# Four graph layers with residual normalisations: one layer's low part taken earlier, one normalisation's moments kept in PSUM

## The reference

```python
x = layernorm(x + hypergraph(x, adj))      # D^-1 H B^-1 H^T (x W1^T) + b, relu, layer norm of 512, once more to 256, + x
x = layernorm(x + relu([x, adj x / deg] W^T))
x = layernorm(x + adj relu(adj relu(adj x V1 + c1) V2 + c2) V3 + c3)
t = relu((adj x) K)
x = layernorm(x + t * (any feature of the node is non-zero))
```

## Time and profile before

| | |
|---|---|
| median of 3 runs | 1506.76 us (1504.32 to 1507.04) |
| the profiled execution's own time | 1506.82 us |
| its span, first to last instruction | 1505.0 us |
| mean granted clock of TensorE | 0.986 of full speed |
| TensorE busy | 1404.5 us, 93% of the span |
| VectorE, ScalarE, GpSimd busy | 78%, 74%, 69% |
| DMA, mean | 31 GB/s |

### The profile page before, as it was taken

One profiled execution on the slowest core, in us unless ns is written; L12 is line 12 of the kernel. 1 busy time (PEld: TensorE's weight loads), 2 busy tenths in 40 slices (PEclk: granted clock), 3 DMA queues, 4 the chain that ended last, 5 costly groups with the idle time before them and its releaser, 6 DMA issues.

```text
span 1505.0 us, 34549 instructions
## 1 busy us (share of the span) xinstructions
PE 1404.5 (93%) x10896; PEld 1350.6 (90%) x10896; DVE 1173.1 (78%) x4060; ACT 1110.5 (74%) x2634; POOL 1038.1 (69%) x1096
## 2 busy tenths in 40 slices
PE   5899999999999999999999999999999999999984
PEld 5799999999999999999999999999999999999974
DVE  5678878878878878878888888888787787887763
ACT  4578777777777777777777777777777777877853
POOL 4676776776776676676676676677677677677642
PEclk8899999999999999999999999999999999999997
DMA  4001001001001101101101101101101101100000
GB/s 132 22 12 36 26 30 36 29 27 36 29 26 36 37 19 37 36 19 37 36 19 37 36 19 37 36 19 37 36 19 36 37 19 36 36 22 22 15 15 22
DMA packets 29956, 47.13 MB, mean 31 GB/s; under 512 B 3408, under 2 KB 12240, under 8 KB 29776
## 3 DMA queue, kind: packets, MB, share of 16 engines
q1 hardware_dynamic: 29776, 44.91, 9.6%
HBM read 28.12 MB, written 16.78 MB: 30 GB/s over the span
## 4 chain that ended last, share of the span: by engine, by line
PE 91%; issue 5%; DVE 2%; ACT 1%; POOL 0%; DMA 0%; POOLq 0%; ACTq 0%; DVEq 0%
PE psum L265 87%; PE psum L382 2%; PE psum L313 1%; DVE n_st L864 1%; DVE p_f L1007 0%; DVE psum L1053 0%; ACT x L574 0%; POOL BH L1258 0%; DVE n_s L1037 0%; DMA at_in<-adjT 0%; DVE psum L1027 0%; DVE x L896 0%; DVE n_mv L869 0%; ACT r_f L579 0%; DVE n_s L1176 0%
## 5 line engine op out<-in xcount | busy, mean ns | idle before, releaser
L1225 POOL TENSOR_TENSOR h_lo<-h_f,h_hi 128x512 fp32r<-128x512 f32 x128 | 166.0, 1297 | 206.1 <-ACT h_hi L555 206.1
L574 ACT ACTIVATE x<-n_s,n_shift,n_rstd 128x256 f32<-128x256 f32 x384 | 208.7, 592 | 3.6 <-DVE n_shift L886 3.2
L1233 POOL TENSOR_TENSOR r_lo<-r_f,r_hi 128x512 fp32r<-128x512 f32 x128 | 163.2, 1302 | 45.3 <-ACT r_hi L555 45.3
L265 PE MATMUL psum<-v_hi,h_hi 128*128 128x256 f32 x512 | 150.3, 294 | 6.8 <-issue 6.8
L864 DVE BATCH_NORM_STATS2 n_st<-n_s 128x6 f32<-128x256 f32 x384 | 142.4, 413 | 9.6 <-POOL n_s L1325 5.2
L1317 POOL TENSOR_TENSOR n_s<-tk,mask 128x512 f32<-128x512 f32 x64 | 66.7, 1042 | 119.5 <-issue 103.8
L265 PE MATMUL psum<-w2c_hi,r_hi 128*128 128x258 f32 x512 | 146.6, 286 | 0.0
L265 PE MATMUL psum<-w2c_lo,r_hi 128*128 128x258 f32 x512 | 145.3, 284 | 0.0
L265 PE MATMUL psum<-v_hi,h_lo 128*128 128x256 f32 x512 | 145.1, 283 | 0.0
L265 PE MATMUL psum<-v_lo,h_hi 128*128 128x256 f32 x512 | 144.8, 283 | 0.0
L265 PE MATMUL psum<-gx_hi,w1T_hi 128*128 128x256 f32 x512 | 144.5, 282 | 0.0
(11 more groups left out here) (159 smaller groups left out, 5524.8 us busy)
## 6 DMA issues: line engine op xcount, KB each, us to landing
x_in<-x_in_dram SPq DMA_DIRECT2D x64, 256.0 KB, 2.8
out<-x SPq DMA_DIRECT2D x64, 256.0 KB, 2.0
at_in<-adjT SPq DMA_DIRECT2D x64, 128.0 KB, 2.5
x<-v_in SPq DMA_DIRECT2D x3, 256.0 KB, 6.0
n_s<-w2T_in SPq DMA_DIRECT2D x2, 256.0 KB, 3.7
r_f<-w1T_in SPq DMA_DIRECT2D x2, 256.0 KB, 4.5
h_f<-wab_in SPq DMA_DIRECT2D x2, 256.0 KB, 6.2
rows<-rows_in SPq DMA_DIRECT2D x1, 256.0 KB, 6.2
```

The source lines that it names most:

```text
L265: return pe.matmul(o, a, b, start=start, stop=stop)
L574: last = act.activation(dst[:, g, :], nm.s[:, g, :], ACT.Identity, scale=nm.rstd[:, g:g + 1], bias=nm.shift[:, g:g + 1])
L1225: return pool.tensor_tensor(dst[1][:], src, f(dst[0][:]), ALU.subtract).then_inc(signal, 1)
L1233: pool.tensor_tensor(r_s[1][:, half], r_f[:, half], f(r_s[0][:, half]), ALU.subtract).then_inc(r_lo[h], 1)
```

## The change

1. `n4`'s moments lie in bank 1 (`BANK["H1"]`) in place of SBUF. So VectorE waits for `h1_relu` of pair `n - 3` before it writes them, and TensorE's `Gx` waits for `n4.shifted`.
2. ScalarE's `root(n4)` stands right behind `root(n3)`, ahead of `square_mean`; it stood behind `round_GT`.
3. VectorE's `invert(n4)` and `shift(n4)` stand right behind `shift(n3)`, ahead of `wide_var`; they stood behind `stats(n2)`.
4. VectorE takes the low part of `Ax3` right behind `sum_n2`. Behind it come `stats(n2)`, the low part of `Gx`, `moments_n2`, `sum_n1` and `stats_alone(n1)`, and only then `invert(n2)` and `shift(n2)`.
5. ScalarE rounds `Ax3` ahead of `round_GT`, and takes `H2`'s relu and rounding ahead of `root(n2)` and `apply(n4)`.

```diff
--- before.py
+++ after.py
@@ -121,7 +121,7 @@
                 self.varied, self.rooted = sem(f"{name}_varied"), sem(f"{name}_rooted")
                 self.inverted, self.done = sem(f"{name}_inverted"), sem(f"{name}_done")
         n1, n2 = Norm("n1", sums=False), Norm("n2", moments=BANK["H1W"])
-        n3, n4 = Norm("n3", moments=BANK["AP3"]), Norm("n4")
+        n3, n4 = Norm("n3", moments=BANK["AP3"]), Norm("n4", moments=BANK["H1"])
         w2T_f = [n3.s[:], n4.s[:]]
 
 
@@ -321,6 +321,8 @@
                     pe.wait_ge(r_relu[0], upto(p - 1))
                 if begun(n - 3):
                     pe.wait_ge(h1_relu, upto(n - 3))
+                if begun(n - 5):
+                    pe.wait_ge(n4.shifted, upto(n - 5))
                 propagate_T("Gx", x_in[:, k % RING], GT[k % 2])
 
             def R(n, k):
@@ -787,6 +789,8 @@
                 if active("AP3", n):
                     p = n - 4
                     root(n3, p)
+                if active("F", n):
+                    root(n4, n - 5)
                 if active("P", n):
                     square_mean(n, k)
                     root_h(n, k)
@@ -808,21 +812,12 @@
                         act.wait_ge(pe_did["H2"], upto(p - 1))
                     copy(h1w[:].rearrange("p g d -> p (g d)"),
                          psum[:, BANK["H1W"], 0:2 * D]).then_inc(h1w_out, 1)
+                if active("Ax3", n):
+                    split_hi("Ax3", ax3, ax3_hi, n - 4, pe_did["TK"])
                 if active("Tr", n):
                     round_GT(n, k)
-                if active("F", n):
-                    root(n4, n - 5)
-                if active("Ax3", n):
-                    split_hi("Ax3", ax3, ax3_hi, n - 4, pe_did["TK"])
                 if active("Gx", n):
                     split_gx(n, k)
-                if active("AXB", n):
-                    root(n2, n - 2)
-                if active("F", n):
-                    p = n - 5
-                    if p >= 2:
-                        act.wait_ge(stored[p % 2], 16 * (p // 2))
-                    apply(n4, p, x4[(k - 5) % 2])
                 if active("H2", n):
                     p = n - 3
                     act.wait_ge(pe_did["H2"], upto(p))
@@ -834,6 +829,13 @@
                     if begun(p - 1):
                         act.wait_ge(pe_did["H2W"], upto(p - 1))
                     copy(h2_s[0][:], h2_f[:]).then_inc(h2_hi, 1)
+                if active("AXB", n):
+                    root(n2, n - 2)
+                if active("F", n):
+                    p = n - 5
+                    if p >= 2:
+                        act.wait_ge(stored[p % 2], 16 * (p // 2))
+                    apply(n4, p, x4[(k - 5) % 2])
                 if active("GP", n):
                     root(n1, n - 1)
                 if active("TK", n):
@@ -1182,12 +1184,16 @@
                 if active("AP3", n):
                     invert(n3, n - 4)
                 if active("F", n):
+                    dve.wait_ge(h1_relu, upto(n - 3))
                     dve.wait_ge(n4.stats, upto(n - 5))
                     dve.memset(wait_pad[:], 0.0)
                     mean_var(n4)
 
                 if active("AP3", n):
                     shift(n3, n - 4)
+                if active("F", n):
+                    invert(n4, n - 5)
+                    shift(n4, n - 5)
                 if active("P", n):
                     wide_var(n, k)
                 if active("P", n):
@@ -1198,23 +1204,21 @@
                     node_degree_recip(n, k)
                     make_agg(n, k)
                     sum_n2(n, k)
-                    stats(n2, n - 2)
-                if active("F", n):
-                    invert(n4, n - 5)
-                    shift(n4, n - 5)
-                if active("AXB", n):
-                    moments_n2(n, k)
                 if active("Ax3", n):
                     dve.wait_ge(ax3_hi, upto(n - 4))
                     split_lo(ax3, flat(BANK["Ax3"]), ax3_lo)
+                if active("AXB", n):
+                    stats(n2, n - 2)
                 if active("Gx", n):
                     split_gx(n, k)
                 if active("AXB", n):
-                    invert(n2, n - 2)
-                    shift(n2, n - 2)
+                    moments_n2(n, k)
                 if active("GP", n):
                     sum_n1(n, k)
                     stats_alone(n1, n - 1)
+                if active("AXB", n):
+                    invert(n2, n - 2)
+                    shift(n2, n - 2)
 
             steps(fill, body)
```

## The result

The changed kernel takes 1439.05 us (median of four runs, 1437.92 to 1440.07); the kernel before took 1506.74 beside it. The ratio is 0.9554, interval 0.9537 to 0.957: 67.7 us less. The prediction said 1454.0 with a range of 1441 to 1474. The sign and the place were right, the size was not: 53 us were expected.

The account below looks back on a forecast made before the run. TensorE was taken to bound the kernel, idling ahead of `TK`. 59 steps of 0.88 us give 52, with 1 from the drain 53: 1506.8 becomes 1453.8, so 1454 us, range 1441 to 1474.

Parts of the forecast that it names:

- The wait ahead of `TK`: TensorE's idle time before `TK`, waiting for VectorE's low part of `Ax3`, goes: 1.02 to 1.10 us a step.
- `n4`'s root, inversion and shift ahead of `wide_var`: On ScalarE and VectorE the three fit in 0.68 us of idle time, cost nothing and leave 0.06.
- Whatever makes `sum_n2` later makes `H2` later, nearly in full: TensorE's `H2` waits for VectorE's `sum_n2`; each 0.1 us later would cost 0.1 a step.
- Moments in PSUM: On VectorE `shift(n4)` took 1.10 us; with PSUM moments it takes 0.16, which makes its move free.
- rival B: VectorE's `HT` comes behind GpSimd's `sq` and waits 0.74 us: 1494, or 1474 in half the steps; chance 0.09.
- C: `n4`'s hand-over between ScalarE and VectorE takes 0.3 us more, losing 0.24 a step: 1468; chance 0.08.
- D: `root(n4)` on ScalarE stands behind something that waits, holding VectorE's `wide_var`: slower, 1528 at 1.3 us; chance 0.03.
- E: No change: something unseen holds TensorE ahead of `TK`, not the low part of `Ax3`: 1506; chance 0.03.
- `xT`'s margin: `x1` is ready 0.9 us ahead of TensorE's `xT`, where it had 0.5 before.
- `H2`'s relu: On ScalarE, placed ahead of `root(n2)` and `apply(n4)`, it delays `root(n1)` by nothing or a tenth.
- `round_GT` behind the rounding of `Ax3`: Later rounding on ScalarE makes GpSimd's `GT_lo` late, and TensorE's `GP` waits for it: 0.20 us a step given back.
- rival A: TensorE's `GP` isn't late, so the 0.20 us doesn't come: 1.08 a step, 65 us, 1442; chance 0.12.

Follow-up runs that it names:

- experiment 6: Kernel before, with only VectorE's low part of `Ax3` moved right behind `sum_n2`; 1469.82 us, ratio 0.975.
- Experiment 3: Changed kernel with one more VectorE instruction, a memset of 256 columns, right ahead of `wide_var` in each step; 1455.42 us, ratio 0.9659.
- experiment 4: Changed kernel with `n4`'s moments back in SBUF, all else as changed; 1450.49 us, ratio 0.9625.
- experiment 7: Kernel before, with `n4`'s shift as two instructions whose second input is a scalar per partition, moments still in SBUF; 1462.43 us, ratio 0.9704.
- experiment 5: Kernel before, with only `n4`'s moments in PSUM and its root, inversion and shift moved behind `n3`'s; 1448.94 us, ratio 0.9609.
- Experiment 1: Changed kernel with ScalarE's `round_GT` moved still later, behind `H2`'s relu and rounding; 1450.14 us, ratio 0.9618.
- experiment 2: Changed kernel with `round_GT` back ahead of the rounding of `Ax3`; 1439.62 us, ratio 0.9551.
- experiment 8: Changed kernel with `H2`'s relu and rounding on ScalarE back behind `root(n2)` and `apply(n4)`; 1461.87 us, ratio 0.9698.

## Why the prediction was wrong in size

Right, by its own steps:

- *The wait ahead of `TK`.* Gone, for 1.02 there (1.82 to 0.80) and 0.08 in `R`. "1.02 to 1.10" was its own figure; the step gained 1.11.
- *`n4`'s root, inversion and shift ahead of `wide_var`.* The shift came 0.12 to 0.28 in the step and `wide_var` at 0.21, in the same place to 0.01 as in experiment 6, where `n4` isn't moved. It cost nothing. It fitted more tightly than the 0.06 left over: no idle time is shown. Experiment 3 gave the price of missing it, one for one.
- *Whatever makes `sum_n2` later makes `H2` later, nearly in full.* 0.25 gave 0.24, and 0.22 gave 0.20 (experiments 3 and 4).
- *Moments in PSUM.* Needed for a free move, as it said: 0.20 a step without. The Trainium skill (SBUF — State Buffer, § Who interferes with whom) says that a VectorE instruction with two SBUF inputs and a GpSimd instruction that reads SBUF shut each other out. The traces agree: with such an instruction running, 1.10 us in the kernel before and 0.36 in experiment 4; 0.16 when it was about done (experiment 6); 0.34 for both parts of the form with one tensor input (experiment 7).
- *`HT`.* 0.28, so rival B did not happen. The hand-over didn't cost more either (C, D), and E is refuted by experiments 5 to 7, each of which shortened the wait by what it did to `ax3_lo`.
- *`xT`'s margin.* `x1` ends at 696.66, 0.79 ahead of `xT`; forecast 0.9.
- *`H2`'s relu: "No cost, or a tenth".* Right as to cost, but its benefit was missed. It is worth 22.8 us given the early low part, 16 of them in the steps.

**The step that failed** is "`round_GT` behind the rounding of `Ax3`": "Now it starts at 721.93 and ends at 722.67. `GP` waits for it. [...] `GP` starts at 722.77 and not at 722.57. So 0.20 is given back". The times of `GT_lo` were about right: it ends 0.18 behind `GP`'s start in the changed kernel. The wait is not there. Two stages of different lag were taken for one pair. `GP` needs the `GT_lo` of the step before, more than 20 us old. Experiment 1 moved `GT_lo` to 2.18 behind `GP`'s start without moving `GP`, and experiment 2 moved it back without any effect. 59 x 0.20 = 12 us of the miss of 15. Without it the forecast's 0.88 would have been 1.08, and the step gained 1.11: another 2 us. The last 1 us is that the forecast started from the profiled execution's time and the result is the median, which lies 1 us under the profiled execution (span 1438.3 and the same 1.8 around it). None of the prediction's signs of being wrong came up (idle time of over 0.3 ahead of `H2`, `xT` or `GP`, a clock below 1.00); the one row that spoke was `GP`, 0.86 to 0.89 behind `H2` and not 1.08. A warning stood in the prediction's own numbers: step 4, with the same TensorE work and no `F`, took 21.48, and the forecast was 21.56, above it, for a wait whose pair had not been written down.

As chances, the 0.12 for rival A was too low. "Against it" stood that `Ax3`'s end is fixed and that the roundings follow each other; both are true and neither bears on what `GP` waits for. And the range stopped at 1441, 1 us below rival A and so with nothing for an error in A's own terms; it missed by 2.

What the runs leave open: whether the long idle time ahead of it is what lowers TensorE's granted clock in the drains of experiments 6 and 8, and how much of the 7.2 and 6.0 us there is the clock. That 0.14 in experiment 1 comes through `x2c` and `apply(n2)` is read from its rows and the code, and was not tried by itself.

None of the eight beats the changed kernel, and experiment 2 equals it. Its step of 21.33 is also what step 4, without `F`, takes (21.34). That no other order could make it shorter isn't shown: the 200.00 of 200.00 can't show it, as said above.

## What to carry to other kernels

In a software pipeline, write the pair beside each name before calling something a wait: a buffer made late in a step is often used only in the next. When one tiny instruction shows a median of 1.10 us and a shortest of 0.16, look at what runs on GpSimd beside it, and first try another form of that instruction; here two lines were worth two thirds of a reordering of three engines. An operand that is taken earlier on one engine makes something else later there, so ask which engine waits for that, and move its work at hand to the front: with the relu back in its old place (experiment 8) the early low part and what was reordered with it cost 13 us more than they brought (experiment 5), about 8 of them in the steps.

## What the runs showed of the hardware

- A VectorE instruction on two SBUF tensors of 128x2 stood until the running GpSimd instruction ended, no longer, even where another followed at once (59 steps of experiment 4, end to end 0.01 to 0.03 us, once 0.11): 0.36 us in experiment 4, from 715.19 to 715.55, with `BH` to 715.53 and `xb` from 715.48 to 716.79.
- The same product with the second operand as a scalar per partition from SBUF didn't stand: 0.34 us for two instructions, inside a GpSimd instruction of 1.28 us.
- `TK` behind a wait shows 0.19 us between its first two matmuls, and 0.12 without one. The wait isn't the only thing that goes with such a gap: `AXB` and `GP`, each right behind a stage of 128x128 matmuls, show 0.20 in the changed kernel with no idle time ahead.
- In a drain, the granted clock of one 10 us stretch was 0.89 in one kernel and 0.51 in another of the same work; twelve matmuls took 1.68 and 2.91 us. Ahead of it TensorE had idled 1.35 us in the first and 3.48 in the second.
